# Splitting weights earlier and interleaving neighbouring tiles' layers in a fused attention and coupling-network kernel

## What is computed

```
q, k, v = xn @ Wq.T, xn @ Wk.T, xn @ Wv.T          # 16 heads of 64
w = sigmoid(q k^T / 8);  w = w / (w.sum(-1) + 1e-6)
attn = (w @ v) @ Wo.T

gf = global_net(mean over the sequence)            # one number for each batch element
out = xn
for _ in range(3):
    tf = sigmoid(gelu(gelu(gelu(out@w1+b1)@w2+b2)@w3+b3)@w4+b4)   # 1024-1024-512-256-1
    c = 0.1 + range * (0.7*gf + 0.3*tf - 0.5) * 2
    out = out + c * twist(out)                     # [o_r,o_i,p_r,p_i] -> [p_r,-p_i,-o_r,o_i]
ffn = out
```

## Time and profile before

| | us |
|---|---|
| two timed runs | 4093.57 and 4131.59, median 4112.58 |
| the profiled execution, its own time | 4120.94 |
| its span, slowest core (core 0) | 4119.4 |
| spans of the other cores | 4035.0 to 4116.2 |
| TensorE busy, core 0 | 3590.0 (87%) |

### The profile page before, as it was taken

How to read it: one execution, slowest core, us unless ns; L and a number is a source line. 1 busy time by engine, 2 the same in 40 slices (tenths; PEclk the granted TensorE clock), 3 DMA queues, 4 the chain that set the end, 5 groups by cost and what they waited for, 6 DMA issues and landing times.

```text
span 4119.4 us, 42346 instructions; the slowest of 8 cores (4035.0 to 4119.4 us)
## 1 busy us (share of the span) xinstructions
PE 3590.0 (87%) x14180; PEld 1797.4 (44%) x14180; DVE 917.1 (22%) x1543; ACT 1068.9 (26%) x2067; POOL 0.2 (0%) x4
## 2 busy tenths in 40 slices
PE   1489999999999999999999999958888888888875
PEld 0233333333333333333333333427766666677662
DVE  4312212222222212222122120031111111111115
ACT  3323323333233233233233331001111111111110
POOL 0000000000000000000000000000000000000000
PEclk9998998988988988989889889978888888888985
DMA  3000000000000000000000000020000000000004
GB/s 93 16 26 1 16 1 1 16 1 1 16 1 1 16 1 1 16 1 16 1 0 16 1 0 11 16 66 7 1 1 1 1 1 1 1 1 1 1 4 161
DMA packets 59912, 54.17 MB, mean 13 GB/s; under 512 B 2242, under 2 KB 53570, under 8 KB 59714
## 3 DMA queue, kind: packets, MB, share of 16 engines
q1 hardware_dynamic: 57410, 43.07, 3.6%
q10 hardware_dynamic: 2304, 8.39, 0.6%
HBM read 43.07 MB, written 8.39 MB: 12 GB/s over the span
## 4 chain that ended last, share of the span: by engine, by line
PE 85%; DVE 6%; ACT 4%; issue 3%; DMA 1%; DVEq 0%; ACTq 0%; SPq 0%
PE p L65 85%; DVE slotA L65 3%; DVE slotC L65 2%; ACT slotC L65 2%; ACT L65 1%; DMA slotB<-x 1%; ACT slotA L65 1%; DVE slotB L65 0%; DMA wblk<-w 0%; ACT wblk L65 0%; ACT g3b L65 0%; ACT tf_sb L65 0%; DVE cp_sb L65 0%; DVEq L55 0%; DMA out<-slotA 0%
## 5 line engine op out<-in xcount | busy, mean ns | idle before, releaser
L65 PE MATMUL p<-slotC 128*128 128x512 f16 (+1 forms) x4096 | 1573.0, 552 | 16.9 <-DVE slotC L65 16.3
L65 PE MATMUL p<-slotA 128*128 128x256 f16 (+1 forms) x6144 | 909.3, 314 | 123.9 <-DVE slotA L65 105.1
L65 PEld LDWEIGHTS p<-slotC 128*128 128x128 f16 (+1 forms) x4096 | 519.8, 130 | 1091.8 <-issue 971.6
L65 PEld LDWEIGHTS p<-slotA 128*128 128x128 f16 (+1 forms) x6144 | 770.6, 126 | 270.3 <-issue 146.6
L65 ACT ACTIVATE slotC<-p 128x512 f32<-128x512 f32 x1024 | 611.5, 597 | 1066.4 <-PE p L65 1066.4
L65 PE MATMUL p<-slotA,slotC 128*128 128x512 f16 x2304 | 505.2, 380 | 25.0 <-DVE slotC L65 24.9
L65 PEld LDWEIGHTS p<-slotA,slotC 128*128 128x128 f16 x2304 | 223.8, 98 | 299.9 <-issue 34.9
L65 PE MATMUL p<-identb,slotC 128*128 128x128 f32 x384 | 143.8, 398 | 224.9 <-ACT slotC L65 124.4
L65 DVE TENSOR_SCALAR slotC<-p 1x512 f32<-1x512 f32 x64 | 43.8, 685 | 1188.9 <-PE p L65 1188.9
L65 DVE RECIPROCAL slotC<-p 64x512 f32<-64x512 f32 x64 | 214.4, 3350 | 109.8 <-PE p L65 109.8
L65 PE MATMUL p<-slotB,wblk 128*128 128x512 f32 x512 | 222.7, 598 | 4.5 <-DVE slotB L65 4.5
(11 more groups left out here) (52 smaller groups left out, 895.3 us busy)
## 6 DMA issues: line engine op xcount, KB each, us to landing
slotB<-x SPq DMA_DIRECT2D x1, 8192.0 KB, 29.7
slotA<-x ACTq DMA_DIRECT2D x16, 512.0 KB, 4.4
out<-slotA SPq DMA_DIRECT2D x16, 512.0 KB, 4.0
wblk<-wqT SPq DMA_DIRECT2D x8, 512.0 KB, 5.2
wblk<-wkT SPq DMA_DIRECT2D x8, 512.0 KB, 4.3
wblk<-wvT SPq DMA_DIRECT2D x8, 512.0 KB, 4.2
wblk<-woT SPq DMA_DIRECT2D x8, 512.0 KB, 4.4
wblk<-w SPq DMA_DIRECT2D x8, 512.0 KB, 4.5
```

The costliest lines, as they stand in the source:

```text
L65: return Inst(getattr(real, op)(*a, **k) if real is not None else None)
```

## The change

Three edits.

1. A pair's weight blocks are loaded and split one pair ahead. The new `load_split_pair` is called for pair 0 ahead of the loop, and for pair p+1 right after pair p's projections, ahead of the attention groups. DVE waits there until PE has ended the projections (`guard_mark`), as these still read the old split weights.
2. The tile loop of the coupling network is rotated. `emit_s16` (the split of a stream tile) and `emit_cn1` are now functions; the first tile's are called ahead of the loop, and those of the next tile stand between cn3 and b7 of the current one.
3. The 16 final additions into `slotC` move into the last cycle, two behind each tile's update. In the same stroke the first additions into `slotB` are cut otherwise: one over the first 256 columns of all 8 chunks, then 8 over the remaining 1792.

```diff
+            def load_split_pair(pair, guard_mark):
                 bq, iq, rq = load_block(wqT, pair, 8, D)
+                V.wait(sT, guard_mark)
                 sqm = split16(bq, iq, rq, *wq16)
...
-                splits = [sqm, skm, svm]
+                return [sqm, skm, svm]
+
+            state["splits"] = load_split_pair(0, 0)
+            for pair in range(NCH):
+                splits = state["splits"]
...
                 att_S = sS.n
+                if pair + 1 < NCH:
+                    state["splits"] = load_split_pair(pair + 1, sT.n)
...
+            V.tensor_tensor(Bv[:, :, 0:FQT], xhv[:, :, 0:FQT], xlv[:, :, 0:FQT],
+                            ALU.add).inc(sV)
...
+            def emit_s16(cy, ti, first=False):
+                t0 = ti * FQT
+                if first:
+                    V.wait(sV, sinit0)
+                else:
+                    V.wait(sT, state["cn1_done"])
+                    V.wait(sV)
...
+            emit_s16(0, 0, first=True)
+            emit_cn1(0, 0)
             for cy in range(3):
                 for ti in range(NFQT):
...
                     g3_ready = sS.n
+                    if nxt is not None:
+                        emit_s16(*nxt)
+                        emit_cn1(*nxt)
 
                     b7 = bacq(7)
...
                     bank_free[6] = [(sV, sV.n)]
+                    if cy == 2:
+                        V.wait(sS, wo_S)
...
+                        for half in range(2):
+                            t = 2 * ti + half
+                            V.wait(sV)
+                            V.tensor_tensor(Cv[:, :, t * 128:(t + 1) * 128],
```

More of the change, by code:

```diff
@@ L356, in emit @@
                      "qrep_done": [0, 0], "qrep_next": None}
-            for pair in range(NCH):
+            def load_split_pair(pair, guard_mark):
                 bq, iq, rq = load_block(wqT, pair, 8, D)
+                V.wait(sT, guard_mark)
                 sqm = split16(bq, iq, rq, *wq16)
@@ L566, in emit @@
             xlv = xn_lo.rearrange("p (c t) -> p c t", c=NCH)
+            V.tensor_tensor(Bv[:, :, 0:FQT], xhv[:, :, 0:FQT], xlv[:, :, 0:FQT],
+                            ALU.add).inc(sV)
+            sinit0 = sV.n
             sinit = []
             for c in range(4):
-                V.tensor_tensor(Bv[:, c, :], xhv[:, c, :], xlv[:, c, :], ALU.add).inc(sV)
-                V.tensor_tensor(Bv[:, c + 4, :], xhv[:, c + 4, :], xlv[:, c + 4, :],
+                V.tensor_tensor(Bv[:, c, FQT:], xhv[:, c, FQT:], xlv[:, c, FQT:],
                                 ALU.add).inc(sV)
+                V.tensor_tensor(Bv[:, c + 4, FQT:], xhv[:, c + 4, FQT:],
+                                xlv[:, c + 4, FQT:], ALU.add).inc(sV)
                 sinit.append(sV.n)
@@ L596, in emit, with emit_cn1 @@
             w1_ready = sV.n
+            strv = Bv
+            Cv = C.ap().rearrange("p (c t) -> p c t", c=NCH)
+            acc_marks = [0] * NTT
+            def emit_s16(cy, ti, first=False):
[5 more added lines that the diff above has]
+                    V.wait(sV)
+                V.tensor_copy(s16h.rearrange("p (c t) -> p c t", c=NCH),
+                              strv[:, :, t0:t0 + FQT]).inc(sV)
+                V.wait(sV)
+                V.tensor_tensor(s16l.rearrange("p (c t) -> p c t", c=NCH),
+                                strv[:, :, t0:t0 + FQT],
+                                s16h.rearrange("p (c t) -> p c t", c=NCH),
+                                ALU.subtract).inc(sV)
+                state["s16_ready"] = sV.n
+            def emit_cn1(cy, ti):
+                for oc in range(NCH):
+                    bi = 4 + oc % 2
+                    b = psum[bi]
+                    T.waits(bank_free[bi])
+                    T.wait(sV, w1_marks[oc])
+                    T.wait(sV, state["s16_ready"])
+                    passes = []
+                    for kc in range(NCH):
+                        lh = w1hi[:, oc * 1024 + kc * 128: oc * 1024 + (kc + 1) * 128]
+                        ll = w1lo[:, oc * 1024 + kc * 128: oc * 1024 + (kc + 1) * 128]
+                        rh = s16h[:, kc * FQT:(kc + 1) * FQT]
+                        rl = s16l[:, kc * FQT:(kc + 1) * FQT]
+                        passes += [(lh, rh), (lh, rl), (ll, rh)]
+                    n = len(passes)
+                    for ip, (lT, rhs) in enumerate(passes):
+                        inst = T.matmul(b[:, 0:FQT], lT, rhs, start=(ip == 0),
+                                        stop=(ip == n - 1))
+                        if ip == n - 1:
+                            inst.inc(sT)
+                    Sc.wait(sT)
+                    Sc.wait(sc_, consts_n)
+                    Sc.activation(g1[:, oc * FQT:(oc + 1) * FQT], b[:, 0:FQT],
+                                  AF.Gelu, bias=cnb1[:, oc:oc + 1]).inc(sS)
+                    bank_free[bi] = [(sS, sS.n)]
+                state["g1_ready"] = sS.n
+                state["cn1_done"] = sT.n
+            emit_s16(0, 0, first=True)
+            emit_cn1(0, 0)
             for cy in range(3):
@@ L600, in emit @@
                     t0 = ti * FQT
[L601 to L641, removed]
+                    g1_ready = state["g1_ready"]
                     for oc in range(4):
@@ L664, in emit @@
                         b = bacq(bi)
-                        T.wait(sf, ffn_w_ready)
                         T.wait(sS, g2_ready)
@@ L699, in emit @@
                     cp_ready = sV.n
[L700 to L712, removed]
                     b6 = bacq(6)
@@ L737, in emit @@
                     bank_free[6] = [(sV, sV.n)]
+                    if cy == 2:
+                        V.wait(sS, wo_S)
+                        if "acc" in tap_marks:
+                            V.waits([tap_marks["acc"]])
+                        for half in range(2):
+                            t = 2 * ti + half
+                            V.wait(sV)
+                            V.tensor_tensor(Cv[:, :, t * 128:(t + 1) * 128],
+                                            Cv[:, :, t * 128:(t + 1) * 128],
+                                            Bv[:, :, t * 128:(t + 1) * 128],
+                                            ALU.add).inc(sV)
+                            acc_marks[t] = sV.n
             ffn_done = sV.n
@@ L757, in emit_xre @@
                 xre_marks[t] = (sxr[t % 2], sxr[t % 2].n)
[L759 to L765, removed]
             emit_xre(0)
```

5 lines of the change are left out of this document (1 added, 4 removed).

## The result

The changed kernel took 0.940 of the kernel before, 95% interval 0.919 to 0.962; the lowest times are 3834.12 us (11 runs) and 4070.13 us (10 runs). I had forecast 4003 us against 4112.6, which is 0.973, with 3958 us as the lower end. 0.940 of 4112.6 is 3867 us: faster, as forecast, but by more than twice the 110 us. The profiled execution of the changed kernel is such a one: cores 4 and 5 were at 0.81 in the groups of all pairs, cores 6 and 7 from 1895 us on. It is read on core 0, which was never at 0.81.

What follows compares the result with a forecast made beforehand. PE's queue was taken as the bound, through its gaps and their effect on the clock. Terms -134 - 20 + 59 - 15 = -110 us took 4112.6 to 4003 us, 2.7% faster, with 3958 to 4050 us for 8 in 10.

Steps and rivals of the forecast that it cites:

- rotation, 23 steps: Coupling network: three PE waits go, step falls from 51.23 to 45.4 us, saving 134 us (ends 95 and 174).
- pairs' start and attention start together: Splits one pair ahead: 20 us saved at pair starts, 59 us lost before attention groups; this edit alone loses 39 us.
- end and start: Final additions moved early save 15 us at the end (10 to 20); network's start loses 0 to 1 us, taken as 0.
- rival A: Coupling network: clock falls in every step as today, 39 us less saved, 4042 us; chance 0.16.
- rival B: Coupling network: clock never falls in the new stretch, 39 us more saved, 3964 us; chance 0.12.
- The attention start: Before attention groups: splits and v block's DMA laid bare, scores 8.4 us later, PE idle 10.5 us, 59 us for 7 pairs.
- The slack of DVE: Coupling network: DVE finishes the next split before the next cn1 is due, by 5 us at the least.
- the 2.55 us left bare: Coupling network: PE's wait for sigmoid and `cp_sb` between b7 and broadcast stays at 2.55 us.
- x's DMA as what is late next at the end: Kernel's end: first output addition waits for the DMA of x, landing at 4021.3, 15 us ahead of 4036.64.
- Rival C: Coupling network: once dense it is granted 0.81, steps take 54.0 us, 4239 us, slower than before; chance 0.05.
- the base of the sum: Whole kernel: the 110 us were taken off the profiled execution's 4120.94 us, giving 4011, then off 4112.6, giving 4003.
- rival D: Attention groups: 0.81 comes in one pair fewer on the slowest core as PE rests longer, 28 us, 3975 us; chance 0.05.

Runs made afterwards that it cites:

- e11: Changed kernel with the first edit undone (rotated network and early end additions only), on a chip without stretches; 0.9651 of the kernel before.
- e6: Kernel before with only the third edit, the 16 final additions in the last cycle; undisturbed spans 3888 to 3901 us.
- e10: Kernel before with only the first edit, weight splits one pair ahead; 1.0078 of the kernel before.
- e1: Kernel before with only the first edit, an earlier run; undisturbed spans 3936 to 3949 us against 3903 to 3921.
- e5: Changed kernel unaltered, run beside the kernel before on one chip; spans without 0.81 of 3799 to 3813 against 3903 to 3920 us, 0.973.
- e12: Kernel before with 16 idle-making DVE instructions ahead of attention groups in pairs 0 to 6, PE resting some 10 us, on a chip with stretches; 0.9757.
- e13: Changed kernel with the first edit undone, on a chip with stretches; 0.986 (0.956 to 1.017) of the kernel before.
- e14: Changed kernel with the next pair's splits in the middle of the second attention group, on a chip with stretches; 3913.40 to 4019.77 us.
- e4: Changed kernel with the next pair's splits in the middle of the second attention group; 0.9592 of the kernel before.
- e9: Kernel before with 16 idle-making DVE instructions ahead of attention groups in pairs 0 to 6, on a chip without stretches; 1.0159 of the kernel before.

## Why the prediction was right and wrong

The working, term by term, on cores without 0.81:

| term | forecast | measured |
|---|---|---|
| rotation, 23 steps | -134 | -120 (e11's -137 less e6's -17) |
| pairs' start and attention start together | +39 | +31 (e10), +34 (e1) |
| end and start | -15 | -17 (e6) |
| sum | -110 | -106 (e10 and e11 added; e5's spans) |

The rotation's step was mis-sized by 0.6 us: I took 45.4 us, the middle of a step without and a step with today's fall, and it is 46.0. That the middle came so near is in part luck, as no row showed a stretch like the new one; the clock falls in each step, as rival A said, but for a shorter time, and rival B fell. The attention start was put 0.5 us too late for each pair: PE rests 10.0 us and not 10.5, since the v block's DMA was waited for 2.25 and not 2.95 us. The slack of DVE, the 2.55 us left bare, and x's DMA as what is late next at the end were right. Rival C did not come true: of the eight couples of the changed kernel that were profiled without a die at 0.81, one shows it in the network (e5, cores 2 and 3, 146 us in all). Its price was added up wrongly too: steps of 54.0 instead of the forecast's 45.4 us give 23 x 8.6 = 198 us and so 4201, not 4239 us.

The step that failed is the base of the sum. "Against the profiled execution's own time that is 4120.94 - 110" kept the 0.81 stretches of that execution as a fixed part of the kernel. They were 4119.4 - 3909 = 210 us of core 0's span, 26 us for each of 8, and in the executions without a die at 0.81 the change takes most of them away. The mechanism stood there as rival D, "because the new gap rests PE longer", but for one pair, 28 us, and with a chance of 0.05. The rows spoke for more: 8 of 8 pairs of core 0 at 0.81, each stretch starting some 4 us after the clock's rise in the groups, and spans of 4119, 4092 and 4036 us with 8, 7 and 5 of them. e12 shows that the rest alone does it, with none in its 28 starts behind the long rest, e13 and e14 that neither the rotation nor the pair's start does. The measured 0.940 is the 0.973 of the work and a difference of a few stretches on the slowest core: from the lowest times, 4070.13 - 3909 = 161 us or 6 stretches before, 3834.12 - 3805 = 29 us or one after. The prediction also left out the executions with a die at 0.81, of which those of the changed kernel took 4180 us and more.

The Trainium skill ("TensorE: Matmul & The Clock Gate", Part 1) has the 0.81 as a limit on the whole die that holds while dense matmuls last. The stretches here held two cores for 161 to 163 us at a time and ended while the same work went on. The spell in the profile of the changed kernel is nearer to that rule, but its cores 4 and 5 were at 0.81 from 227 us on and cores 6 and 7 only from 1895 us on.

What stays open: why a rest of 10 us keeps the stretches away. It is not a matter of the one start alone. The last pair has the short rest in the kernels with the long one too, and there it shows no stretch in 20 starts, where the kernels with the short rest everywhere show 12 in 24. Nor was the rest told apart from the low clock that comes with it: 1.2 GHz for 13.7 and 17.1 us at the starts of two pairs of the changed kernel, for 6.8 us before. Whether the long rest makes a die at 0.81 more frequent was not settled either. It had couples above 9 counts in 8 of 14 executions of the changed kernel in the first measurement, chip C speaks for it (5 of 11 executions against none of 13), and on chip B the shares are alike; chips and moments differ. So the gain beyond the work, 0.940 instead of 0.973, is shown for executions without a die at 0.81 and is no promise for the average one.

## What to carry to other kernels

Before a sum is made against a profiled execution, split its time into work and granted clock: read the clock over the long stretches of all cores, see whether spans differ by whole multiples of something, and price the change against a core that shows none. Count such stretches in the traces and not in the spans alone, and look at the executions that a ratio leaves out. When a step is moved ahead of a wait, look for a place where its engine has time and nobody queues behind it: the same six splits cost 56 us between projections and attention (e4 against the changed kernel) and nothing that shows in the middle of a group. Work moved beside a wait should be put inside it, as a wait that stays whole next to small matmuls keeps its price in idle time and in clock.

## What the runs showed of the hardware that was not expected

- A granted clock of 0.81 that sets in 3 to 6 us after the clock's rise at the start of attention groups or of `Wo`, mostly lasts 161 to 163 us and ends while PE's work goes on unchanged, and costs some 26 us in the groups and 30 us in `Wo`; it comes on couples of cores (0 and 1, 2 and 3, and so on) together, on three of the five chips of the experiments in each execution of the kernel before, on one in none of nine.
- No such stretch behind 140 pair starts with a rest of 10 us, and 67 behind 192 with a rest of 2 us.
- 62 us of added rest with which a kernel takes 0.976 (0.959 to 0.993, e12) on such a chip, where the same kernel takes 1.016 on another (e9).
- A clock that falls to 1.2 GHz in a stretch of 4.2 us between dense matmuls with b7 and the broadcast in it, in each of 23 steps, and not at all once these two stand inside cn1 (0.94 against 1.00 over 840 us).
